# Four graph layers on one core: layer 2's normalisation on ScalarE as scale and shift, with a new order on all engines

## The reference

```python
x = _layernorm(x + _L0_gnn_ref(x, adj, adj, ...))   # 8-head attention with edge bias and mask
x = _layernorm(x + _L1_gnn_ref(x, adj, ...))        # two convolutions, distance-weighted sum, GRU gate
x = _layernorm(x + _L2_gnn_ref(x, adj, ...))        # one-head attention: exp(e_i + f_j) weighted by adj
x = _layernorm(x + _L3_gnn_ref(x, adj, ...))        # 4-head attention, leaky ReLU, masked softmax
```

## Time and profile before

| | |
|---|---|
| median of 3 runs | 1408.46 us (1406.12 to 1408.89) |
| the profiled execution, its own time | 1408.24 us |
| its span, first to last instruction | 1406.5 us |
| mean granted TensorE clock | 0.98 of full speed |
| TensorE matmul busy | 1344.6 us, 96% |
| TensorE weight load busy | 1043.0 us, 74% |
| VectorE busy | 1212.4 us, 86% |
| ScalarE busy | 1185.0 us, 84% |
| GpSimd busy | 596.5 us, 42% |
| DMA queue 1 | 44.27 MB, 10.0% of 16 engines |

### The profile page before, as it was taken

One profiled execution on the slowest core, in us unless ns is written; L12 is line 12 of the kernel. 1 busy time (PEld: TensorE's weight loads), 2 busy tenths in 40 slices (PEclk: granted clock), 3 DMA queues, 4 the chain that ended last, 5 costly groups with the idle time before them and its releaser, 6 DMA issues.

```text
span 1406.5 us, 40636 instructions
## 1 busy us (share of the span) xinstructions
PE 1344.6 (96%) x13330; PEld 1043.0 (74%) x13330; DVE 1212.4 (86%) x3407; ACT 1185.0 (84%) x4450; POOL 596.5 (42%) x918
## 2 busy tenths in 40 slices
PE   6799999999999999999999999999999999999974
PEld 3577778877777877777787777787777778777753
DVE  7658889889999988999888999989898999888874
ACT  6877888988888998888898888889888888986664
POOL 1123444544344444435344434445443444545532
PEclk8999999999999999999999999999999999999995
DMA  3101010001011011101101101110110111000000
GB/s 134 31 31 32 31 32 31 17 32 39 16 40 39 25 38 39 32 24 39 39 24 39 40 17 38 39 39 24 39 39 17 39 39 32 24 17 31 9 16 24
DMA packets 23826, 46.88 MB, mean 33 GB/s; under 512 B 2753, under 2 KB 2754, under 8 KB 23490
## 3 DMA queue, kind: packets, MB, share of 16 engines
q1 hardware_dynamic: 23618, 44.27, 10.0%
HBM read 35.88 MB, written 8.39 MB: 31 GB/s over the span
## 4 chain that ended last, share of the span: by engine, by line
PE 89%; ACT 4%; DVE 4%; issue 2%; POOL 1%; DVEq 0%; POOLq 0%; ACTq 0%
PE B L708 18%; PE B L605 17%; PE B L508 14%; PE B L548 5%; PE B L572 4%; PE B L618 3%; PE B L519 2%; PE B L534 2%; PE B L761 2%; PE B L789 2%; PE B L662 2%; PE B L702 2%; PE B L827 2%; PE B L595 2%; PE B L773 2%; PE B L679 2%
## 5 line engine op out<-in xcount | busy, mean ns | idle before, releaser
L1019 ACT ACTIVATE e<-B,nm 128x128 f32<-128x128 f32 x1024 | 362.7, 384 | 12.8 <-DVE nm L1387 12.8
L508 PE MATMUL B<-ident,e 128*128 128x128 f32 x1536 | 233.5, 279 | 17.2 <-ACT pT L1028 8.8
L1377 DVE SCALAR_TENSOR_TENSOR B<-an,rowb,mask 128x512 f32<-128x512 f32 x256 | 190.6, 789 | 50.9 <-ACT h L1152 42.2
L1019 ACT ACTIVATION_READ_ACCUMULATOR e<-B,nm 128x1 f32 x1024 | 231.0, 226 | 0.0
L508 PEld LDWEIGHTS B<-ident,e 128*128 128x128 f32 x1536 | 178.8, 143 | 35.9 <-issue 12.3
L1177 ACT ACTIVATE e<-l,nm 128x128 f32<-128x128 f32 x512 | 198.7, 402 | 5.5 <-DVE nm L1616 5.5
L377 POOL TENSOR_TENSOR veps<-meanv,eps 128x4 f32<-128x4 f32 x128 | 26.4, 206 | 399.6 <-DVE meanv L1350 399.6
L1387 DVE TENSOR_REDUCE nm<-B 128x4 f32<-128x512 f32 x256 | 168.7, 673 | 26.2 <-PE B L548 26.0
L1028 ACT ACTIVATE pT<-B 128x512 f32<-128x512 f32 x256 | 155.6, 620 | 1.7 <-PE B L508 1.7
L380 POOL TENSOR_TENSOR rstd<-veps,neghalf 128x4 f32<-128x4 f32 x128 | 130.0, 1016 | 10.0
L391 POOL TENSOR_TENSOR xs<-xs 128x288 f32<-128x288 f32 x32 | 40.8, 1276 | 203.6 <-ACT xs L1059 203.6
(11 more groups left out here) (200 smaller groups left out, 3423.5 us busy)
## 6 DMA issues: line engine op xcount, KB each, us to landing
xt<-in_x_t SPq DMA_DIRECT2D x32, 256.0 KB, 3.4
an<-in_adj_n SPq DMA_DIRECT2D x32, 256.0 KB, 2.9
xn<-in_x_n SPq DMA_DIRECT2D x32, 256.0 KB, 3.0
at<-in_adj_t SPq DMA_DIRECT2D x32, 256.0 KB, 2.7
out_x<-xo SPq DMA_DIRECT2D x32, 256.0 KB, 3.3
wm<-in_mats SPq DMA_DIRECT2D x1, 1088.0 KB, 9.1
wm<-in_mats SPq DMA_DIRECT2D x1, 832.0 KB, 6.7
wm<-in_mats SPq DMA_DIRECT2D x1, 320.0 KB, 2.9
```

What stands on the lines that cost most here:

```text
L508: last = mm(g(dst, b), g(src, b), ident[:, :], is_transpose=True, start=(b == 0), stop=True, skip_group_check=True)
L1019: last = fn(g(e0[:, h % 2, :], b), g(bank, b), ACT.Exp, bias=nm0[:, h % 4, b:b + 1], accum_out=sum0[s % 2][:, b, head(h):head(h) + 1])
L1377: v.scalar_tensor_tensor(out=bank[:, :], in0=an[s % AN][:, :], scalar=we[:, head(h):head(h) + 1], in1=mask0[:, :], op0=ALU.mult, op1=ALU.a ...
```

## The change

Layer 2's normalisation goes from VectorE to ScalarE. GpSimd makes a second small tile, shift = -mean * rstd, and ScalarE computes `x * rstd + shift` with its Identity function, with both as operands from tiles, in four instructions of 128 columns. The order of the helpers is new on ScalarE, VectorE, TensorE, GpSimd and SyncE, and several helpers use other banks with other lists of users. All offsets grow by seven, with seven more steps. The work of every other helper is unchanged. Cut to its core:

```diff
+ON_ACT = (2,)
-STEPS = GROUPS + 46
+STEPS = GROUPS + 53
+        negone = sb("negone", [128, GB])
+        shift = {i: sb(f"shift{i}", [128, GB]) for i in ON_ACT}
+        ln_shift = {i: sem(f"ln_shift{i}") for i in ON_ACT}
@@ SyncE
             def step(t):
-                load_xt(t)
-                load_at(t - 2)
+                store(t - 11)
+                load_at(t - 5)
+                load_xn(t - 2)
+                load_xt(t - 1)
                 load_an(t)
-                load_xn(t)
-                store(t - 10)
@@ GpSimd, rsqrt
                 pool.tensor_tensor(rstd[i][:, :], veps[i][:, :], neghalf[:, :], ALU.pow)\
                     .then_inc(ln_rstd[i], 1)
+                if i in ON_ACT:
+                    pool.tensor_tensor(shift[i][:, :], meanv[i][:, :, 0], negone[:, :], ALU.mult).then_inc(ln_shift[i], 1)
+                    pool.wait_ge(ln_rstd[i], s + 1)
+                    pool.wait_ge(ln_shift[i], 2 * s + 1)
+                    pool.tensor_tensor(shift[i][:, :], shift[i][:, :], rstd[i][:, :], ALU.mult).then_inc(ln_shift[i], 1)
@@ GpSimd, step
-                rsqrt(0, t - 41)
-                spread_sums(t - 40)
-                rsqrt(2, t - 43)
-                z_parts(t - 42)
-                z_times_x(t - 42)
+                spread_sums(t - 47)
+                rsqrt(0, t - 48)
+                rsqrt(2, t - 50)
+                z_parts(t - 49)
+                z_times_x(t - 49)
@@ TensorE, step (lists of users left out, but one)
-                gate_z, values 0, sums_T, probs_T 0, values 1, project_v, probs3_T 1, gate_hn, x1_T, hidden3,
-                probs_T 1, probs_T 2, gate_in, conv1, scores 1, probs3_T 2, x3_T, probs3_T 3 (B[7]), project_out (B[1])
+                gate_z, sums_T, values 0, probs_T 0, project_v, values 1, probs3_T 1, gate_hn, probs_T 1, x1_T,
+                hidden3, probs_T 2, gate_in, conv1, probs3_T 2, scores 1, x3_T, probs3_T 3 (B[1]), project_out (B[7])
-                project_out(t - 39, B[1], (("n_ready", -2, 1, 1), ("exp_done", 1, 8, 3),
-                    ("ln_out1", -3, 1, 1), ("m1_done", -2, 1, 1), ("dd_ready", -2, 1, 1),
+                project_out(t - 46, B[7], (("hp_ready", -1, 1, 1), ("pT_ready", 1, 8, 2),
+                    ("pT_ready", 1, 8, 1), ("pT_ready", 0, 8, 8), ("pT3_ready", -4, 4, 1),
+                    ("em_ready", -2, 1, 1), ("v2_done", -2, 1, 1), ("dd_ready", -2, 1, 1),
                     ("res0_done", -1, 1, 1)))
@@ ScalarE
+            def ln_apply(i, s, src, dst):
+                act.wait_ge(ln_shift[i], 2 * s + 2)
+                for b in range(GB):
+                    last = fn(g(dst, b), g(src, b), ACT.Identity, scale=rstd[i][:, b:b + 1], bias=shift[i][:, b:b + 1])
+                last.then_inc(ln_out[i], 1)
+
+            def norm2(s):
+                ...
             def step(t):
-                ...
-                keep_probs(t - 40, 7, B[5])
-                tanh_r(t - 42, B[3])
-                exps3(t - 44, 2)
-                exps(t - 39, 0, B[6])
-                exps(t - 39, 1, B[4])
-                ...
+                exps3(t - 51, 0)
+                exp_edges(t - 50)
+                leaky(t - 51, 2, B[0])
+                affinity(t - 49, (B[7], B[5], B[3], B[2]))
+                exps3(t - 51, 1)
+                ...
+                exps3(t - 51, 2)
+                keep_probs(t - 47, 7, B[7])
+                tanh_r(t - 49, B[3])
+                exps(t - 46, 0, B[4])
+                exps(t - 46, 1, B[6])
+                ...
+                exps(t - 46, 3, B[2])
+                keep_probs(t - 46, 2, B[0])
+                norm2(t - 50)
+                tanh_n(t - 49, B[1])
+                conv_input(t - 48, B[7])
@@ VectorE, step, from hidden_times_e to the fourth seed
-                hidden_times_e(t - 41), norm1, row_max3 2, edge_mask, divide3, seed_edges 0, 1, 2, row_scales, seed_edges 3
-                norm2(t - 42) stood after seed_edges 5 to 7, norm3 ahead of hidden_times_e, aggr0 after residual2
+                hidden_times_e(t - 48), norm1, aggr0, row_max3 2, norm3, divide3, seed_edges 0, 1, row_scales,
+                seed_edges 2, 3; edge_mask stands behind seed_mask3 1
```

More of the change, by code:

```diff
@@ L838, in step @@
             def step(t):
[L839 to L843, removed]
+                gate_r(t - 48, B[3], (("n3_done", -3, 1, 1), ("em_ready", 0, 1, 1), ("kh1_ready", 3, 1, 1),
+                    ("l3_done", -2, 4, 1), ("exp_done", 2, 8, 5), ("recT_ready", 1, 1, 1),
+                    ("tr_ready", -1, 1, 1)))
@@ L849, in step @@
[L849 to L855, removed]
@@ new lines, in ln_apply @@
+            def ln_apply(i, s, src, dst):
[4 more added lines that the diff above has]
+            def norm2(s):
+                if not live(s):
+                    return
+                wait(act, q["x3t_ps"], s - 1)
+                wait(act, q["r3_done"], s - 1)
+                ln_apply(2, s, r2, x3[s % 2])
@@ new lines, in step @@
+            def step(t):
+                exps3(t - 51, 0)
[3 more added lines that the diff above has]
+                exps3(t - 51, 1)
+                keep_probs3(t - 51, 0, B[7])
+                conv_relu(t - 49, B[6])
+                keep_q(t - 46, B[0])
+                keep_gathered(t - 49, B[2])
+                leaky(t - 51, 3, B[1])
+                exps3(t - 51, 2)
[3 more added lines that the diff above has]
+                exps(t - 46, 1, B[6])
+                tanh_z(t - 49, B[0])
+                keep_sums(t - 47, B[3])
+                exps(t - 46, 2, B[1])
+                keep_probs(t - 46, 0, B[7])
+                keep_v(t - 46, B[0])
+                keep_probs3(t - 51, 1, B[4])
+                exps3(t - 51, 3)
+                keep_probs(t - 46, 1, B[7])
+                keep_x1(t - 48, B[5])
+                keep_h3(t - 51, B[4])
+                exps(t - 46, 3, B[2])
[3 more added lines that the diff above has]
+                conv_input(t - 48, B[7])
+                keep_probs3(t - 51, 2, B[0])
+                keep_x3(t - 50, B[2])
+                keep_probs3(t - 51, 3, B[1])
+                exps(t - 46, 4, B[3])
+                keep_ej(t - 50, B[2])
+                keep_d(t - 48, B[7])
+                keep_out3(t - 51, B[1])
+                keep_probs(t - 46, 3, B[0])
+                exps(t - 46, 5, B[6])
+                squares(t - 48)
+                exps(t - 46, 6, B[4])
+                keep_probs(t - 46, 4, B[0])
+                keep_probs(t - 46, 5, B[1])
+                message_relu(t - 48)
+                exps(t - 46, 7, B[5])
+                leaky(t - 50, 0, B[3])
+                leaky(t - 50, 1, B[6])
+                keep_probs(t - 46, 6, B[2])
+                keep_k(t - 45, 0, B[3])
+                keep_k(t - 45, 1, B[3])
@@ new lines, in step @@
+                row_max(t - 45, 2, B[1])
+                aggr2(t - 49)
+                residual3(t - 51)
+                half_tanh(t - 48)
+                norm0(t - 47)
+                row_max(t - 45, 3, B[2])
+                seed_edges(t - 45, 4, B[3], (("recT_ready", -1, 1, 1), ("tr_ready", -3, 1, 1),
+                    ("n3_done", -6, 1, 1), ("em_ready", -3, 1, 1), ("kh1_ready", 0, 1, 1),
+                    ("l3_done", -5, 4, 1), ("exp_done", -1, 8, 5)))
+                divide(t - 46, B[5])
@@ new lines, in step @@
+                seed_edges(t - 45, 7, B[5], (("x1T_ready", -2, 1, 1), ("oT_ready", -1, 1, 1),
+                    ("r2_done", -4, 1, 1), ("em_ready", -3, 1, 1), ("hb_done", -4, 1, 1),
+                    ("exp_done", -1, 8, 8)))
+                z_times_n(t - 48)
+                row_max(t - 45, 4, B[3])
+                invert_sums3(t - 50)
+                residual0(t - 46, B[7])
+                row_max(t - 45, 5, B[6])
+                gru_out(t - 48)
+                stats0(t - 46)
+                row_max(t - 45, 6, B[4])
```

395 lines of the change are left out of this document (163 added, 232 removed).

## The result

The changed kernel takes 1427.76 us (median of 4 runs, 1426.62 to 1430.46) against 1408.35 us for the kernel before on the same chip. The ratio is 1.0137, 95% interval 1.0123 to 1.0151: slower by 19.4 us. I had said 1421.5, range 1405 to 1431.

A forecast was written before the change was run, and what follows sets the result against it. TensorE, busy 96% of the span, was taken as the bound, with no cover for delays. Span 1406.5 + 12.2 (27 periods x 0.45) + 1.2 (drain) = 1419.9 us, own time 1421.6, forecast 1421.5; range 1405 to 1431.

The forecast's parts named there:

- Bound and slope: TensorE bounds the 41.30 us period; nothing that delays it has cover, so a wait there lengthens the period.
- Part 2: Norm2 on ScalarE: four ACTIVATEs take 1.54 us, conv_input ends at +19.64, project_out waits; +12.2 us in all.
- the term of 0.45 at `project_out`: TensorE's project_out waits for conv_input to free bank 7, about 0.45 us in each of 27 periods.
- Parts 1 and 3: Norm2 leaving VectorE is worth nothing by itself; the shift on GpSimd adds some 0.7 us, hidden in the period.
- Part 4: VectorE's new order: the fourth seed ends at +2.7, scores starts at +2.75; they touch, put at zero.
- rival B: A second stall: scores waits 0.3 us for VectorE's seeds in each of 27 periods, 8.1 more, 1429.6; chance 0.12.
- Part 5: Other bank swaps free at least 0.1 us ahead of their takers; SyncE's five transfers behind one wait stay hidden.
- Part 6: In the drain norm2 stands alone on the path; shift 0.7 and longer ACTIVATEs 0.5 add 1.2 us, once.
- The fill: The time before the steady periods, taken as unchanged, with a bound of a microsecond or two either way.
- The sum: Span 1406.5 + 12.2 + 1.2 = 1419.9 us, own time 1421.6; forecast 1421.5, chance 0.47.
- Rival A: Norm2's four ACTIVATEs take 0.77 to 1.15 us, TensorE never waits, only the drain's 1.2 stays: 1409.6; chance 0.24.
- Rival C: Faster: project_k's wait, 0.40 us a period, vanishes, 10.8 less, 1398; or 2 to 4 less in fill and drain; chance 0.17.

The follow-up runs named there:

- e1_norm2_dve: The changed kernel with its new order, but norm2 back on VectorE and no shift on GpSimd; 1410.34 us, ratio 1.001.
- e4_eight: The changed kernel with norm2's four ScalarE instructions done twice, the first time into a spare tile; 1478.82 us (one run).
- e10_ej_first: The changed kernel with two of head 4's four exponentials moved behind keep_ej on ScalarE; 1422.2 us, ratio 1.0095.
- e5_swap: The changed kernel with the transposes y_T moved behind logits3 on TensorE; 1433.41 us, ratio 1.0159.
- e6_dve_swap: The kernel of e1_norm2_dve with y_T moved behind logits3 on TensorE; 1415.03 us, ratio 1.0031.
- e3_one_act: The changed kernel with norm2 as one ScalarE instruction of 512 columns instead of four of 128; 1417.28 us, ratio 1.005.

## Why the prediction was right, and where it wasn't

- *Bound and slope.* Right. TensorE had no cover, and 1.54 us on ScalarE turned into 0.47 us a period (expected 0.45). e1_norm2_dve gives 41.35 without, the changed kernel 41.79 with it, e4_eight 43.33 with twice as much.
- *Part 2, price and places.* The four ACTIVATEs took 1.54 us, the value of the `squares` rows. Exps 0 starts at 755.59, +4.79 (I had 4.84), `keep_probs3(1)` at +11.23 (I had 11.37), `conv_input` ends at +19.46 (I had 19.64). So the term of 0.45 at `project_out` was mis-sized: it measured 0.16 there and 0.10 at the transposes behind it, 0.26. The other step that failed is where I stopped: I followed the late stretch as far as `conv_input`. `keep_ej`, 3 us further on the same stretch, holds `conv_both` for another 0.21, which I had at nothing; e10_ej_first shows it. That 0.26 + 0.21 comes out next to my 0.45 is luck. `x3_T`, which needs norm2's result, I also left out; it was about 0.2 us from being late and cost nothing here, and it takes nearly all of the loss in e4_eight.
- *Parts 1 and 3.* Right: VectorE takes norm2 back in e1_norm2_dve for 0.05 us a period at most, and the shift is hidden in the steady periods, where norm2 follows `keep_probs` 2 at once (766.87 to 767.34).
- *Part 4 and rival B, the seeds.* It was close, and didn't happen. `scores` starts at 753.47, +2.67, not late, and no TensorE wait ends on the seeds; e1_norm2_dve, with the same VectorE stretch there, has a period only 0.05 above before.
- *Part 5.* Right on SyncE: it now waits once for the third masks, and nobody waits for `at`. The wait of `mask_a` ends on `affinity`. Wrong on the banks, which I had free 0.1 us ahead of each taker: the third `probs3_T`, put ahead of `scores` 1, waits in each period for `keep_probs` 2, with norm2 on either engine (0.99 or 1.00 behind `conv1`, where the same transposes follow a product of that size after 0.86 elsewhere). The whole order costs only 0.05 a period all the same.
- *Part 6, the drain.* Mis-sized: 1.2 us said, 4.0 measured, 3.75 of it from norm2's place (table of the spans). The chain of waits of the changed kernel near the end:

```profile
1337.33 0.94 ACT x L1203 x3
...
1368.58 1.00 ACT x L1203 x3
...
1390.90 1.01 POOL rstd L385
1393.22 1.26 ACT x L1203 x3
1394.62 1.95 PE B L518 x8
```

  In the last group the power's end to the transposes takes 1394.62 - 1391.91 = 2.71 us against 1.38 in e1_norm2_dve (norm2 follows the power at once): +1.3, the 1.2 that I had. But in the drain norm2 stands on the chain for earlier groups too, which I had not looked for (1337.33, 1368.58): the two periods up to 1359.91 are 33.97 and 32.65 us long against 33.43 and 31.55 in e1_norm2_dve, 1.6 more. In the second of them `x3_T` waits for norm2's result, idle for 0.48 us and 1.08 behind its neighbour against 0.44. The first period of the drain takes the steady 0.44, the stretch after 1359.91 takes 1.67, the 1.3 among it. So it is also wrong that the stall goes in the drain.
- *The fill.* I took it as unchanged, within 2 us. In the profiled executions it differs by 5 us, in those of the other kernels with the new order (e4_eight aside) by 0.9 to 3.9. How much of it is the order stays open; by the medians, e1_norm2_dve against before, all that the order costs is 1.6 us, of which 26 x 0.05 = 1.3 are the period.
- *The sum.* I had 13 us more and 19.4 came. By the spans, 1.2 of the missing 6.4 lie in the 26 periods, 2.4 in the drain, and the rest ahead of the periods and in the scatter of the runs; the time lies in the range because that had room for rival B, which didn't happen.
- *Rival A, no new stall.* False as a price (0.385 us per instruction, not 0.19), and the rule cited for it did not hold here. The Trainium skill (Perfetto Trace Analysis, Identifying the Most-Contended Engine) calls matmul busy time a bad measure of how close TensorE is to its limit and weight-load busy time a better one, by which TensorE had room: 32.2 of 41.8 us. As a forecast of what a wait costs the trace speaks against it here: e4_eight's 1.54 us came out as 1.53.
- *Rival C, faster.* `project_k`'s wait of 0.18 is still there in each period. Its premise was also wrong in a way that I couldn't see: e5_swap took the wait away and e6_dve_swap most of it, and the period stayed, because `distances` and, in e5_swap, `conv_own` came next with nothing to spare.
- *The other rule cited.* The Trainium skill (ScalarE: Activation LUTs, Rules for kernel authors) puts adds and multiplies on VectorE. The runs agree: with norm2 on VectorE this order is 17.4 us faster.

## What to carry to other kernels

When an instruction is put into an in-order stream, list everybody who waits for it or for what stands behind it, its own result first, and go past the first taker to each one until the stream idles: here the first late taker had 0.26 us and the next one another 0.21. A busy share of 86% says nothing about it. A wait that is taken away is worth only the distance to the next chain that is just as late: before moving something past it, walk from the moved instruction through its readers to the banks that they free. Read spacings of TensorE's starts against the same neighbours in another trace, since bank waits of 0.1 to 0.2 us left no idle mark here, and one of 0.4 a mark of 0.18. And compare with a kernel that has the same order without the suspect: a late taker in the right stretch can be the order's, as the third `probs3_T` was.

## What I hadn't expected of the hardware

An ACTIVATE from SBUF to SBUF with both operands from tiles costs 0.385 us from start to start for 128 columns, and 0.70 for 512 (e3_one_act). Four small ones against a big one are 1.54 to 0.70, so more than half of what norm2 costs on ScalarE goes with the number of instructions.

A bank passes from ScalarE to TensorE in 0.05 to 0.06 us: 767.49 to 767.54, 770.26 to 770.32 and 773.44 to 773.50 in the changed kernel's period above. So a hand-over can be followed to a tenth of a microsecond, while the idle column shows nothing for any of the three.
